# A new order of the five engines' steps in the pipelined attention part of a decoder layer

## The reference

```python
x = _layernorm(x + _L0_attn_ref(x, ...), axis=-1)
x = _layernorm(x + _L0_xattn_ref(x, ctx_1024, ctx_1024, ...), axis=-1)
x = _layernorm(x + _L0_ffn_ref(x, L0_ffn_w_gate, L0_ffn_w_up, L0_ffn_w_down), axis=-1)
# within _L0_xattn_ref, 16 heads of 16 features
sm = jnp.einsum('nlhd,nshd->nlhs', q, k) / math.sqrt(D)
sm = jax.nn.softmax(sm, axis=1)
attn = jnp.einsum('nlhs,nshd->nlhd', sm, v).reshape(N, L, H * D)
```

## Time and profile before

| | us |
|---|---|
| median of 3 runs | 1104.57 |
| lowest and highest | 1101.99, 1105.56 |
| the profiled execution | 1103.74 |
| its span in the trace | 1101.9 |
| TensorE, ScalarE, VectorE, GpSimd busy | 1004.1, 891.0, 892.7, 533.8 |

### The profile page before, as it was taken

One profiled execution on the slowest core, in us unless ns is written; L12 is line 12 of the kernel. 1 busy time (PEld: TensorE's weight loads), 2 busy tenths in 40 slices (PEclk: granted clock), 3 DMA queues, 4 the chain that ended last, 5 costly groups with the idle time before them and its releaser, 6 DMA issues. The chain is left out here.

```text
span 1101.9 us, 28772 instructions
## 1 busy us (share of the span) xinstructions
PE 1004.1 (91%) x7910; PEld 854.6 (78%) x7910; DVE 892.7 (81%) x1983; ACT 891.0 (81%) x3030; POOL 533.8 (48%) x588
## 2 busy tenths in 40 slices
PE   1468999999999999999999999999779989797997
PEld 0357888888888888888888888877469978686897
DVE  7346888888888888888888888888645689899698
ACT  1367999999999999999999999997526699553894
POOL 0123456555565565546554655564400067677243
PEclk9989999999999999999999999999779999999799
DMA  6127766677677766776667667764300000000233
GB/s 180 50 75 207 201 185 192 191 203 193 175 201 194 196 179 191 197 192 188 186 193 204 187 181 198 204 185 121 86 9 0 1 1 1 1 0 1 65 106 96
DMA packets 138145, 149.15 MB, mean 135 GB/s; under 512 B 17282, under 2 KB 137826, under 8 KB 138088
## 3 DMA queue, kind: packets, MB, share of 16 engines
q1 hardware_dynamic: 136128, 148.04, 47.9%
q10 hardware_dynamic: 1960, 0.42, 0.3%
HBM read 94.47 MB, written 53.94 MB: 135 GB/s over the span
## 5 line engine op out<-in xcount | busy, mean ns | idle before, releaser
L668 ACT ACTIVATE Ps<-score,nmax_s 112x112 f32<-112x112 f32 x512 | 174.8, 399 | 10.7 <-DVE nmax_s L862 10.7
L576 POOL TENSOR_TENSOR Ph<-Px 125x448 f32<-125x448 f32 x128 | 146.4, 1144 | 72.0 <-ACT Px L687 69.5
L679 ACT ACTIVATE Px<-score,nmax_h 125x112 f32<-125x112 f32 x512 | 172.6, 369 | 0.7 <-DVE nmax_h L855 0.3
L593 POOL TENSOR_TENSOR Vn<-Vx,rZc 125x128 f32<-125x128 f32 x192 | 77.0, 402 | 188.3 <-DVE x L951 85.8
L855 DVE TENSOR_REDUCE nmax_c<-score 125x8 fp32r<-125x896 f32 x128 | 138.9, 1085 | 20.3 <-PE score L1139 19.3
L583 POOL TENSOR_TENSOR Ps<-Ps,rZs 112x896 f32<-112x896 f32 x64 | 107.7, 1683 | 83.2 <-DVE rZs L900 42.1
L687 ACT ACTIVATE Px<-score 125x896 f32<-125x896 f32 x128 | 119.7, 935 | 17.7 <-PE score L1150 9.8
L1139 PE MATMUL score<-QxS,KxS 96*125 96x224 f32 x768 | 128.1, 290 | 3.8 <-DMA QxS<-Qx_parts 2.3
L668 ACT ACTIVATION_READ_ACCUMULATOR Ps<-score,nmax_s 112x1 f32 x512 | 129.5, 253 | 0.0
L1139 PEld LDWEIGHTS score<-QxS,KxS 96*125 96x125 f32 x768 | 103.2, 191 | 22.0 <-issue 11.1
L679 ACT ACTIVATION_READ_ACCUMULATOR Px<-score,nmax_h 125x1 f32 x512 | 114.3, 223 | 0.0
(11 more groups left out here) (229 smaller groups left out, 3051.1 us busy)
## 6 DMA issues: line engine op xcount, KB each, us to landing
KxS<-Kx_parts SPq DMA_DIRECT2D x192, 187.5 KB, 3.4
Kx_parts<-Kx SPq DMA_DIRECT2D x64, 375.0 KB, 3.9
ctx_in<-in_ctx SPq DMA_DIRECT2D x32, 375.0 KB
KsS<-Ks_parts SPq DMA_DIRECT2D x192, 56.0 KB, 2.2
QsS<-Qs_parts SPq DMA_DIRECT2D x96, 112.0 KB, 3.0
QxS<-Qx_parts SPq DMA_DIRECT2D x192, 56.0 KB, 3.5
Ks_parts<-Ks SPq DMA_DIRECT2D x32, 224.0 KB, 1.9
Qs_parts<-Qs SPq DMA_DIRECT2D x32, 224.0 KB, 3.1
```

What stands on the lines that cost most here:

```text
L576: pool.tensor_tensor(Ph[p][:], Px[u % NPX][:, :, 0:L // 2], Px[u % NPX][:, :, L // 2:L], ALU.add)\
L593: pool.tensor_tensor(Vn[u % NPX][:], Vx[n.par][:, c, P * t:P * (t + 1)].rearrange("s (h e) -> s h e", h=OCT), rZc[u % NPX][:].rearrange("s ...
L668: ins = act.activation(Ps[:, g, :], score[slot][0:L, h // QUAD, (h % QUAD) * L:(h % QUAD + 1) * L], ACT.Exp, bias=nmax_s[:, g:g + 1], accu ...
L679: ins = act.activation(Px[u % NPX][:, h, :], score[SLOT_OF[f"C{u}"]][0:C, h // QUAD, (h % QUAD) * L:(h % QUAD + 1) * L], ACT.Exp, bias=max ...
```

## The change

All batches' stage numbers rise by one: STAGES is 8, and n7 is what n6 was. Two operations move to another stage against the rest: `save_x2` is done one step later, `load_ctx` one step earlier. The operations themselves, their shapes and their number stay. The order within the step is another on each of the five queues, and the uses are spread over the three banks in another way, with other neighbours (7, 6 and 9 uses instead of 8, 7 and 7). The slots of the scores keep their order. In the diff below the old orders of GpSimd, ScalarE, VectorE and TensorE are left out, since they stand in the functions above.

```diff
--- before.py
+++ after.py
@@ -68,7 +68,7 @@
 
 
 
-STAGES = 7
+STAGES = 8
 FIRST = 1 - STAGES
 LOOP_FROM = 2
 LOOP_PAIRS = (B - STAGES - LOOP_FROM) // 2
@@ -76,13 +76,13 @@
 
 
 WORK_USES = (
-    (("xT", 6), ("ctxT1", 4), ("V0", 4), ("V1", 4), ("Qs", 6), ("K1", 4), ("PT0", 5), ("ctxT0", 5)),
-    (("AVs1", 4), ("Vs", 5), ("Ox", 1), ("K0", 4), ("PT1", 5), ("PT3", 5), ("PT2", 5)),
-    (("AVs0", 4), ("Os", 4), ("Ks", 6), ("x2T", 0), ("V2", 4), ("x1T", 4), ("Qx", 4)),
+    (("ctxT0", 5), ("xT", 7), ("Qs", 7), ("K0", 5), ("V1", 5), ("V2", 5), ("PT2", 6)),
+    (("PT3", 5), ("AVs1", 5), ("Vs", 6), ("Ks", 7), ("K1", 5), ("PT0", 6)),
+    (("AVs0", 5), ("Os", 5), ("ctxT1", 5), ("Ox", 2), ("V0", 5), ("x2T", 1), ("x1T", 5), ("Qx", 5), ("PT1", 6)),
 )
 SLOT_USES = (
-    (("S0", 5), ("C0", 3), ("C2", 3), ("C4", 3)),
-    (("C5", 2), ("S1", 5), ("C1", 3), ("C3", 3)),
+    (("S0", 6), ("C0", 4), ("C2", 4), ("C4", 4)),
+    (("C5", 3), ("S1", 6), ("C1", 4), ("C3", 4)),
 )
 WORK_OF = {use: bank for bank, uses in enumerate(WORK_USES) for use, _ in uses}
 SLOT_OF = {unit: slot for slot, uses in enumerate(SLOT_USES) for unit, _ in uses}
@@ -530,29 +530,30 @@
                 wait(sp, scores_c, read)
                 lay_on_diagonal(n, "Qx", QxS, PARTS_OF_Q, qx_laid)
 
-            def step(n0, n1, n2, n3, n4, n5, n6):
-                if n6:
-                    load_x(n6)
-                if n3:
-                    lay_keys_cross(n3, 0)
-                    save_keys_cross(n3, 1)
-                    lay_queries_cross(n3)
-                    lay_keys_cross(n3, 1)
-                if n6:
-                    save_keys_self(n6)
+            def step(n0, n1, n2, n3, n4, n5, n6, n7):
+                if n7:
+                    load_x(n7)
+                if n4:
+                    save_keys_cross(n4, 1)
                 if n0:
                     save_x2(n0)
-                if n5:
-                    load_ctx(n5)
-                if n6:
-                    save_queries_self(n6)
-                    lay_keys_self(n6)
                 if n4:
-                    save_keys_cross(n4, 0)
-                if n6:
-                    lay_queries_self(n6)
+                    lay_keys_cross(n4, 0)
+                    lay_queries_cross(n4)
+                if n7:
+                    load_ctx(n7)
+                    save_queries_self(n7)
                 if n4:
-                    save_queries_cross(n4)
+                    lay_keys_cross(n4, 1)
+                if n7:
+                    save_keys_self(n7)
+                    lay_queries_self(n7)
+                if n5:
+                    save_keys_cross(n5, 0)
+                if n7:
+                    lay_keys_self(n7)
+                if n5:
+                    save_queries_cross(n5)
             iterations(sp, step)
             sp.wait_ge(x2_saved, 16 * B)
 
@@ -612,33 +613,35 @@
...
+            def step(n0, n1, n2, n3, n4, n5, n6, n7):
+                if n3:
+                    normalise_values(n3, 1)
+                    normalise_values(n3, 2)
+                    halve_cross(n3, 3)
+                if n1:
+                    inverse_root(n1, 1)
+                if n3:
+                    halve_cross(n3, 5)
+                if n6:
+                    add_output_bias(n6)
+                if n3:
+                    normalise_values(n3, 3)
+                    normalise_values(n3, 4)
...
+                    add_output_bias_2(n4)
+                if n6:
+                    normalise_probs(n6, 0)
+                if n5:
+                    inverse_root(n5, 0)
+                if n4:
+                    halve_cross(n4, 0)
+                if n3:
+                    normalise_values(n3, 5)
+                if n6:
+                    normalise_probs(n6, 1)
+                if n4:
+                    normalise_values(n4, 0)
+                    halve_cross(n4, 2)
             iterations(pool, step)
...
         @block.scalar
@@ -758,54 +761,54 @@
...
+            def step(n0, n1, n2, n3, n4, n5, n6, n7):
+                if n5:
+                    copy_probs(n5, 2)
+                    copy_probs(n5, 3)
+                    copy_probs(n5, 1)
+                    hi_context(n5, 0)
+                if n3:
+                    exp_shifted(n3, 3)
+                if n5:
+                    even_self(n5, 0)
+                    even_self(n5, 1)
+                if n3:
+                    exp_by_head(n3, 4)
+                if n6:
+                    copy_values_self(n6)
+                if n7:
+                    copy_xT(n7)
+                if n5:
+                    hi_context(n5, 1)
+                if n3:
+                    exp_shifted(n3, 5)
+                if n7:
+                    hi_queries_self(n7)
+                if n6:
+                    exp_self(n6, 0)
+                if n7:
+                    hi_keys_self(n7)
+                if n6:
+                    exp_self(n6, 1)
+                if n5:
+                    hi_keys_cross(n5, 0)
+                if n1:
+                    copy_x2T(n1)
...
+                    exp_shifted(n4, 0)
+                if n5:
+                    copy_x1T(n5)
+                    hi_keys_cross(n5, 1)
+                if n4:
+                    exp_by_head(n4, 1)
+                if n5:
+                    hi_queries_cross(n5)
+                if n4:
+                    exp_shifted(n4, 2)
...
+                    copy_probs(n6, 0)
+                if n3:
+                    even_cross(n3)
             iterations(act, step)
...
         @block.vector
@@ -957,90 +960,89 @@
...
+            def step(n0, n1, n2, n3, n4, n5, n6, n7):
...
+                    sum_cross(n3, 2)
+                    max_cross(n3, 4)
+                    reciprocal_cross(n3, 2)
+                if n5:
+                    pick_self(n5, 0)
+                if n1:
+                    mean_variance(n1, 1)
+                if n5:
+                    pick_self(n5, 1)
+                if n3:
+                    max_cross(n3, 5)
+                if n5:
+                    lo_context(n5, 0)
+                    residual(n5, 0)
+                if n1:
+                    add_eps(n1, 1)
+                if n3:
+                    sum_cross(n3, 3)
+                if n5:
+                    moments(n5, 0)
+                if n1:
+                    norm_cross(n1)
+                if n6:
+                    max_self(n6, 0)
+                if n5:
+                    lo_context(n5, 1)
+                    mean_variance(n5, 0)
+                if n7:
+                    lo_with_bias(n7, "Qs", Qs, bcol["abq"], qs_hi)
+                if n3:
+                    reciprocal_cross(n3, 3)
+                if n6:
+                    max_self(n6, 1)
+                if n3:
+                    reciprocal_cross(n3, 4)
+                if n2:
+                    residual(n2, 1)
+                if n5:
+                    add_eps(n5, 0)
+                if n6:
+                    reciprocal_self(n6, 0)
+                if n3:
+                    sum_cross(n3, 5)
+                if n7:
+                    lo_with_bias(n7, "Ks", Ks, bcol["abk"], ks_hi)
...
+                    max_cross(n4, 0)
+                if n5:
+                    values_with_bias(n5, 0)
+                if n1:
+                    largest(n1)
+                if n5:
+                    norm_self(n5)
+                if n3:
+                    reciprocal_cross(n3, 5)
+                if n5:
+                    lo_keys_cross(n5, 0)
+                if n4:
+                    max_cross(n4, 1)
+                if n5:
+                    values_with_bias(n5, 1)
+                if n6:
+                    reciprocal_self(n6, 1)
+                if n4:
+                    max_cross(n4, 2)
+                if n5:
+                    lo_keys_cross(n5, 1)
+                if n4:
+                    sum_cross(n4, 0)
+                    reciprocal_cross(n4, 0)
+                if n5:
+                    values_with_bias(n5, 2)
+                if n2:
+                    moments(n2, 1)
+                if n5:
+                    lo_with_bias(n5, "Qx", Qx, bcol["xbq"], qx_hi)
+                if n4:
+                    reciprocal_cross(n4, 1)
+                    max_cross(n4, 3)
             iterations(dve, step)
...
         @block.tensor
@@ -1207,79 +1209,78 @@
...
+            def step(n0, n1, n2, n3, n4, n5, n6, n7):
+                if n5:
+                    transpose_probs(n5, 3)
+                if n3:
+                    shift(n3, 3)
+                if n5:
+                    transpose_ctx(n5, 0)
+                if n3:
+                    cross_values(n3, 0)
+                    cross_values(n3, 1)
+                if n5:
+                    self_values(n5, 0)
+                    self_values(n5, 1)
+                if n3:
+                    cross_values(n3, 2)
+                    cross_scores(n3, 5)
+                if n5:
```

(48 more changed lines are left out.)

221 lines of the change are left out of this document (9 added, 212 removed).

## The result

The kernel after took 1095.3 us (median of 4 runs, 1094.85 to 1096.23), the kernel before 1105.07 us in the same rounds; the ratio is 0.9914, 95% interval 0.9898 to 0.9931. It is 0.9% faster; 1097.7 was forecast. The profiled execution took 1095.15 us with a span of 1093.4.

A forecast was written before the change was run, and what follows sets the result against it. TensorE and ScalarE, both nearly full, were taken as the bound; ScalarE's smaller gain, 0.25 us over 27 steps, gave 6.8 us, with fill and drain 0: 1097.7 us on the median scale, range 1087 to 1112.

The forecast's parts named there:

- What bounds it: Steady part: TensorE and ScalarE both nearly full; order can give at most ScalarE's idle of 0.78 us a step.
- Rival (a): Steady part: ScalarE's new waits are as long as those removed, so no change, 1104.6 us; chance 0.19.
- The sum: Steady step: TensorE gains 0.44 us, ScalarE 0.25; the smaller decides, 27 steps give 6.8 us.
- the walk: One steady step followed through the five queues in the new order, using old durations; ScalarE's waits came to 0.53 us.
- the first move: TensorE: shift(.., 5) ahead of transpose_x gains 0.17 us a step; ScalarE's copy_xT newly waits 0.23.
- one like the second: The second: ScalarE's hi_queries_self ahead of exp_self(.., 0) fills its 0.38 us idle; point reached 0.18 us sooner.
- rival (c): Steady part: all ScalarE idle but the branch's 0.2 us goes, 15.7 us saved, 1089 us; chance 0.12.
- (b): Steady part: cross_scores(.., 1) begins late, exp_by_head(.., 1) waits one for one; slower, 1115 us; chance 0.17.
- GpSimd's pause at 0: GpSimd after inverse_root: pause falls to about 1 us, gaining nothing because normalise_values(.., 3) had 1.8 us of cover.
- Landings at 0: DMA in the steady part: moved transfers gain nothing; QxS landing keeps about 2.5 of 3 us to spare.
- The fill at 0 with 3 us to either side: Fill and drain: no net change, 3 us either way, since orders suiting full steps may suit empty ones badly.
- Rival (d): Drain: the forecast plus a second clock drop costing 2.8 us, 1100.5 us, shown by low clock before 778; chance 0.10.

The follow-up runs named there:

- before_shift5_first: Kernel before with one TensorE swap, shift(n2, 5) ahead of transpose_x(n6); ratio 0.9985, 22.25 us a step.
- before_c1_later: Kernel before with one TensorE swap, cross_scores(n3, 1) behind shift(n3, 0); ratio 1.0186, 22.92 us a step.
- before_keys_first: Kernel before with ScalarE's hi_keys_self(n6) copied ahead of exp_self(n5, 0); ratio 1.0024, 22.28 us a step.
- before_pause_short: Kernel before with VectorE's norm_cross(n0) moved ahead of max_self(n5, 0), to shorten GpSimd's pause; ratio 0.9996, 22.29 us a step.
- before_unrolled: Kernel before with its loop written out, no branch, order unchanged; ratio 0.9971 to before, 22.04 us a step.
- after_unrolled: Kernel after with its loop written out, no branch, order unchanged; ratio 0.9921 to before, 21.75 us a step.
- after_sp_old: Kernel after with SyncE's transfers in the old order, load_ctx and save_x2 at their old stages; ratio 0.9961 to before.
- after_rc2_first: Kernel after with one VectorE swap, reciprocal_cross(n3, 2) ahead of max_cross(n3, 4); ratio 0.9887 to before, median 1091.75 us.
- after_rc2_unrolled: Kernel after with VectorE's reciprocal_cross(n3, 2) ahead of max_cross(n3, 4) and the loop written out; ratio 0.9920 to before.
- after_cut_back: Kernel after with its order kept but the step boundary and loop branch moved back to their old place; ratio 0.9927 to before.

## Right or wrong, step by step

- **What bounds it.** Not contradicted, and half shown. Freeing TensorE alone gave nothing in the steady part (before_shift5_first). before_c1_later cost at once, but it held TensorE as well as ScalarE. Taking ScalarE's own wait away gave nothing either (before_keys_first), which fits that run's rival, that the two hold each other.
- **Rival (a), no change.** Out: the interval of the ratio, 0.9898 to 0.9931, doesn't reach 1.
- **The sum.** 0.25 us a step was forecast for the order, 0.28 is what the unrolled pair shows; 27 x 0.25 = 6.8 us, and 24 steady steps gave 6.8. ScalarE's idle was to be 0.53 and is 0.49, the step near 22.0 and is 21.82, the busy share over 97.5% and is 97.8%. That the parts agree so well is partly luck, for the 0.49 isn't made of the walk's parts. Of its five waits (0.23, 0.06, 0.07, 0.10, 0.07) one is found, `copy_xT`'s, at 0.13, and the last is 0.2 us in the whole stretch. The largest listed, ScalarE's for `transpose_probs` (`ACT PsT <- PE work`, 5.4 us, 0.21 a step), stands nowhere in the walk, which took the new spread of `copy_probs` for a gain alone. Also, done alone, the first move gave 0 and one like the second -0.05. They aren't additive, and which combination makes the 0.28 stays open.
- **The term left out.** The walk carried the branch along unchanged, and rival (c) took it for a fixed 0.2. It had a price of 4.8 us in all in before, and 3.2 of them went, 2.2 to 2.4 by the place of the cut and the rest by the order. This is the steady part's excess over the forecast.
- **The waits.** `exp_self` for nmax_s was to be under 4 us and isn't listed any more; those of TensorE for ctxT_lo and Ps are gone, the one for Kx has moved to the cross projections (4.0 us). The new wait of `copy_xT` was priced at 0.23 a step, 3.2 us in 18 times were found (0.13). `exp_by_head` for nmax_h has 0.2 us: (b) is refuted, its premise with it, since `cross_scores(.., 1)` wasn't late. TensorE's loads for Vn, where the walk allowed up to 0.1 a step, went from 5.5 to 9.6 us, 0.16 a step.
- **GpSimd's pause at 0.** Right for before, as far as before_pause_short tests it. The 69.2 us of the earlier trace rows are 14 times out of 25; in the other steps the same idle is named for rZc, as in the earlier trace rows. Without the loop the profile names all 25. This wait in 140 to 700 us, in before_unrolled and then in after_unrolled:

```profile
POOL Vn L588 <- DVE x L946: 122.2, 25, 5.7
```

```profile
POOL Ph L572 <- DVE x L949: 40.6, 25, 1.6
```

  The idle behind the root is thus 4.9 us a step before and 1.6 after, where "about 1" was forecast; "69.2 under 25" came true (4.9) only by which engine the profile names, three times in 25. Incomplete for after: there the shortness is a condition of the order, and the "cover of 1.8 us" belonged to the old sequence.
- **Landings at 0.** Right in the steady part (after_sp_old). QxS in the drain: 1.8 us instead of 2.3.
- **The fill at 0 with 3 us to either side.** The +2.7 us lie inside, but the larger part of their cause, the clock, was weighed for the drain alone, and the queue of the transfers wasn't weighed for the fill at all.
- **Rival (d).** The drop came before 778 us, as (d) said it would:

```profile
772.00:807.00 35.00, 26.12 (x136) 16.30 (x129) 19.12 (x51) 12.36 (x44) 9.12 (x16) 0.51 0.08 20
```

  (kernel after; before has 0.73 in these 35 us). As a sign it was a weak one: the clock fell at 772.5 instead of 781.6 us, but 7.3 of these 9.1 us are only that the 25th x2T copy came that much sooner. It stayed low until 806.7 us without the break that before had. Against before nothing is lost: the seven last steps take 108.0 us against 108.1. Beside profiles of its own order the price shows. At a mean granted clock of 0.87 in these steps after, after_rc2_first and after_rc2_unrolled take 107.1 to 108.1 us; at 0.90 after_sp_old and after_unrolled take 106.5, and at 0.94 after_cut_back 106.0. So the longer low clock cost after some 1 to 2 us, not 2.8, and the -0.1 hides a drain that the new order made shorter by about as much. The 2.8 was taken from two neighbouring steps of the drain, 15.4 and 20.5 us, which differ in their work too: in after they are 17.5 and 19.8, with nearly all of the first ahead of the low clock.
- **Rival (c).** ScalarE's idle didn't go down to the branch's 0.2; the time fell between the forecast and (c).

In sum the median is 2.4 us below the forecast. In the profiles it is -3.2 (branch), -1.1 (feed-forward part), -0.1 (drain) and +2.7 (fill), together -1.7; the other 0.7 is how the profiled executions lie to their medians. That the branch's excess and the fill's loss nearly cancel is luck. The -1.1 isn't the change's doing as far as is known: the same untouched part takes 292.4 to 296.5 us in the fourteen profiles.

## What to carry to other kernels

Where several queues are full, don't price an order by the waits that it removes: none of the moves tried alone in the kernel before gained, and two cost. Treat the place at which a loop's step is cut as a choice of its own; writing the loop out once tells what the branch costs. Look at the first pass through a reordered pipeline separately: a copy that hides a wait in a full step only delays an empty one. And before a wait's total is compared between two kernels, count how often it is named: once a step, or only where that engine happened to come last.

## What the runs showed of the hardware

- One loop branch over five queues cost 4.8 / 11 = 0.44 us an iteration in one order and 1.6 / 11 = 0.15 in the other. Most of it isn't a row of its own: on ScalarE the rows of a step fill 21.33 us without the branch and 21.46 with it (before_unrolled and before), and one row of VectorE is named `issue`.
- The column of the granted clock can miss a stretch. after_rc2_first in 68 to 76 us:

```profile
68.00:76.00 8.00, 6.63 (x32) 4.19 (x31) 1.97 (x5) 2.47 (x7) 0.72 (x1) 1.00 0.01 2
```

  Its clock reads 1.00, yet the products are these, as long as in after at 0.50:

```profile
71.80 2.04 PE L1111 MATMUL work<-aWo,attnT 128*112 128x256 f32 x4 [0.83 <-DVE attnT L910]
73.64 1.91 PE L1111 MATMUL work<-aWv,xT 128*112 128x256 f32 x4
```

  The durations of like products are the safer sign.
- ScalarE's rows overlap their successors by 0.1 to 0.2 us, and like copies differ in length (the 25 of x2T in after from 382 to 497 ns). Busy shares of 96.7% and 97.1% in 300 to 500 us went with steps of the same length (before, before_shift5_first).
- In the drain of the new order the last seven steps took 106.0 us at a mean granted clock of 0.94, 106.5 at 0.90 and 107.1 to 108.1 at 0.87.
